# Second expert layer, block stage: GpSimd issues the 24 weight transfers instead of ScalarE

## The reference, cut to what matters

```python
E, K, F = (8, 2, 352)
scores = jax.nn.softmax(logits, axis=-1)
topk_w, topk_i = jax.lax.top_k(scores, K)
topk_w = topk_w / (topk_w.sum(-1, keepdims=True) + 1e-20) * SCALE
combine = jnp.zeros((T, E), jnp.float32).at[jnp.arange(T)[:, None], topk_i].set(topk_w)
g = jax.nn.silu(jnp.einsum('td,edf->etf', x, w_gate)) * jnp.einsum('td,edf->etf', x, w_up)
expert_out = jnp.einsum('etf,efd->etd', g, w_down)
y = jnp.einsum('te,etd->td', combine, expert_out).astype(x.dtype)
return y + _swiglu_mlp(identity, sw_gate, sw_up, sw_down)
```

## Time and profile before

| | us |
|---|---|
| median of 3 runs | 3525.72 |
| lowest and highest of them | 3525.45, 3530.16 |
| the profiled execution | 3523.55 |
| its span, first to last instruction | 3522.0 |
| block stage, first DMA issue to last result copy | 3055.65 to 3380.45 |

### The profile page before, as it was taken

How to read it: one execution, slowest core, us unless ns; L and a number is a source line. 1 busy time by engine, 2 the same in 40 slices (tenths; PEclk the granted TensorE clock), 3 DMA queues, 4 the chain that set the end, 5 groups by cost and what they waited for, 6 DMA issues and landing times. The chain is left out here.

```text
span 3522.0 us, 56185 instructions
## 1 busy us (share of the span) xinstructions
PE 3188.7 (91%) x17981; PEld 2290.7 (65%) x17982; DVE 2037.6 (58%) x4470; ACT 1273.8 (36%) x1786; POOL 1626.9 (46%) x933
## 2 busy tenths in 40 slices
PE   5875999999539999999999999999999957699988
PEld 4655888888536666666666666666666555477766
DVE  5656555555746666666766766666666662122235
ACT  2332333333434444444444444444444432122222
POOL 5002333333235666655666655666656636500037
PEclk8995999999769999999999999999999958899999
DMA  4000000001451111111111101111010031421223
GB/s 110 1 1 9 14 13 9 13 9 57 162 214 46 52 45 46 53 45 35 61 45 54 45 27 69 45 54 45 27 69 28 7 106 64 140 68 63 63 70 109
DMA packets 89978, 192.94 MB, mean 55 GB/s; under 512 B 12768, under 2 KB 58152, under 8 KB 83760
## 3 DMA queue, kind: packets, MB, share of 16 engines
q1 hardware_dynamic: 74864, 162.28, 13.1%
q0 software_dynamic: 10816, 21.07, 2.1%
q10 hardware_dynamic: 4224, 8.65, 0.7%
HBM read 137.60 MB, written 54.30 MB: 54 GB/s over the span
## 5 line engine op out<-in xcount | busy, mean ns | idle before, releaser
L2070 POOL TENSOR_TENSOR d_acc<-d_acc,d_pr 128x1024 f32<-128x1024 f32 x384 | 938.2, 2443 | 91.1 <-ACT d_pr L1974 60.4
L1974 ACT ACTIVATE d_pr<-d_p 128x1024 f32<-128x1024 f32 x512 | 487.0, 1026 | 236.2 <-PE d_p L1909 236.2
L1843 PE MATMUL d_pO<-d_pr,d_V 128*64 128x512 f32 x2048 | 473.0, 599 | 0.0
L2070 POOL TENSOR_TENSOR d_acc<-d_pr 128x1024 f32<-128x1024 f32 x64 | 153.1, 2392 | 620.9 <-ACT d_pr L1974 620.9
L2019 DVE TENSOR_REDUCE d_nm<-d_p 128x2 f32<-128x1024 f32 x256 | 304.6, 1222 | 94.9 <-PE d_p L1886 94.9
L2014 DVE CUSTOM_DVE_ANT_0 d_biased<-d_p,d_masked 128x512 f32<-128x512 f32 x512 | 330.6, 688 | 31.8 <-issue 31.8
L935 POOL TENSOR_TENSOR e_hs<-e_hf,e_hs 128x512 fp32r<-128x512 f32 x136 | 175.6, 1291 | 365.4 <-ACT e_hs L910 365.4
L1843 PEld LDWEIGHTS d_pO<-d_pr,d_V 128*64 128x64 f32 x2048 | 135.4, 136 | 261.5 <-issue 235.0
L965 DVE SCALAR_TENSOR_TENSOR res<-e_pY,m_Wt,res 128x256 f32<-128x256 f32 x544 | 225.9, 478 | 44.6 <-PE e_pY L871 43.8
L2030 DVE RECIPROCAL d_rb<-d_rb 128x128 f32<-128x128 f32 x256 | 224.6, 920 | 7.5 <-ACT d_rb L1967 7.5
L871 PEld LDWEIGHTS e_pY<-e_Wd,e_hs 128*128 128x128 f32 x1632 | 213.5, 191 | 13.8 <-POOL e_hs L935 2.2
(11 more groups left out here) (287 smaller groups left out, 5628.2 us busy)
## 6 DMA issues: line engine op xcount, KB each, us to landing
d_W<-w_split SPq DMA_DIRECT2D x32, 1536.0 KB, 6.4
kv_split<-c_ys SPq DMA_DIRECT2D x16, 1024.0 KB, 5.7
d_kv<-kv_split SPq DMA_DIRECT2D x8, 2048.0 KB, 10.6
d_masked<-mask_bias SPq DMA_DIRECT2D x64, 256.0 KB
x_slots<-m_zeros SPq DMA_DIRECT2D x1, 9088.0 KB, 29.7
b_x<-x_slots SPq DMA_DIRECT2D x71, 128.0 KB, 2.0
y_slots<-b_y SPq DMA_DIRECT2D x71, 128.0 KB, 1.7
w_split<-w_parts SPq DMA_DIRECT2D x4, 1536.0 KB, 5.3
```

What stands on the lines that cost most here:

```text
L1843: last = pe.matmul(pO[own[h], :], V[vb][:, s, par * P + h * HD1:par * P + (h + 1) * HD1], pr[:, s % PT, h, :], start=(s == 0), stop=(s == ...
L1974: act.activation(pr[:, n % PT, :, :], slot(st, what, n)[:, :, :], ACT.Exp).then_inc(exp_done, 1)
L2070: pool.tensor_tensor(acc[:, q, :, :], a, pr[:, s % PT, :, :], ALU.add).then_inc(acc_done, 1)
```

## The change

POOL issues the 24 weight transfers, and ACT issues none. POOL issues those of experts 0 and 1 first. Then, for each expert e, it issues those of expert e+2 (while there is one) and after that waits for expert e and marks it. Neither the transfers themselves, their semaphores, their order nor any wait of PE is changed.

```diff
             @block.gpsimd
             def _(pool):
+                def load(e):
+                    pool.dma_start(wgu[:, e, :, :], io["r1_gu"][:, e]).then_inc(w_in[e], 16)
+                    pool.dma_start(wd[:, e, 0:2, :], io["r1_d"][e, 0:2 * P].rearrange("(f p) d -> p f d", p=P)
+                                   ).then_inc(w_in[e], 16)
+                    pool.dma_start(wd[0:F1 - 2 * P, e, 2, :], io["r1_d"][e, 2 * P:F1]).then_inc(w_in[e], 16)
+
+                load(0)
+                load(1)
                 for e in range(E1):
+                    if e + 2 < E1:
+                        load(e + 2)
                     pool.wait_ge(w_in[e], 48)
                     pool.memset(told[:, e:e + 1], 0.0).then_inc(w_ready, 1)
...
             @block.scalar
             def _(act):
-                for e in range(E1):
-                    act.dma_start(wgu[:, e, :, :], io["r1_gu"][:, e]).then_inc(w_in[e], 16)
-                    act.dma_start(wd[:, e, 0:2, :], io["r1_d"][e, 0:2 * P].rearrange("(f p) d -> p f d", p=P)
-                                  ).then_inc(w_in[e], 16)
-                    act.dma_start(wd[0:F1 - 2 * P, e, 2, :], io["r1_d"][e, 2 * P:F1]).then_inc(w_in[e], 16)
-
```

## The result

| | before | after |
|---|---|---|
| median of 20 runs, us | 3525.46 | 3518.24 |
| lowest and highest | 3522.57, 3530.16 | 3513.43, 3524.32 |
| profiled execution, its span | 3523.55, 3522.0 | 3518.08, 3516.5 |

The ratio is 0.998, with a 95% interval of 0.9974 to 0.9986: faster by 7.2 us, where 12.3 were forecast. The time lies inside the stated range (3510 to 3519), close to its upper end, and just past the 7.1 us at which the prediction put the bound to no change.

The account below looks back on a forecast made before the run. PE's late start, set by ACT's list of DMA issues, was taken to bound the block stage, a fixed PE run of 305.3 us. First product 12.3 us earlier: 3525.72 - 12.3 = 3513.4 us, range 3510 to 3519.

Parts of the forecast that it names:

- the likeliest case: The forecast itself: gain 10.4 to 13.5 us, time 3512.2 to 3515.3, chance 0.68.
- rivals 1 and 2: POOL or its queue slower, gain 7.4 us, chance 0.12; blocks slower beside the weights, gain 6.3, chance 0.08.
- The start of PE: Block stage: PE's first product at 3062.9 instead of 3075.16, a gain of 12.3 us.
- The two bounds that were weighed: Mark 0 comes at the later of POOL finishing nine issues (3062.3) and expert 0's data landing (3062.5).
- POOL's issues: Ahead of mark 0: an expert's three issues take 2.13 us, nine 6.39, plus 0.27 for the first.
- I carry the same 305.3 us: First product to last result copy: the 71 blocks take as long as before, 305.3 us.
- Rival 2: Blocks run slower beside the weights: late row loads stall PE twice, 3.0 us each; gain 6.3, 3519.4 us; chance 0.08.
- The slack: SP's row loads: landing in 5.8 us at worst, needed after two blocks, 8.6 us; slack of 2.8 us.
- The clock: Block 0 again runs at the lower level (1.2 GHz); a rise one block later costs up to 3.8 us more.
- Later marks: POOL's marks after expert 0: up to 2.1 us later than their data, costed at nothing, covered by the blocks' length.
- Rivals 1 and 3: Nine POOL issues at 1.3 us, gain 7.4, chance 0.12; mark 0 behind stalled issues, up to 3549 us, chance 0.12.
- The two-port rule of the third rival: DVE in a two-port mode blocks GpSimd's DMA descriptors: nine issues 27.9 us, run 3534.5 us; chance 0.01.

Follow-up runs that it names:

- e5: The kernel before, with ACT's first copy of turned rows moved up behind expert 0's three transfers, ahead of the other 21; 3522.98 us, ratio 0.9994.
- e7: The changed kernel, with result stores issued by ACT and POOL pausing ahead of the loads of experts 3 to 7; 3512.83 us, ratio 0.9965.
- e6: The changed kernel, with POOL issuing all 24 transfers ahead of its first mark instead of nine; 3523.02 us, ratio 0.9992.
- e2: The changed kernel, with result stores issued by ACT behind its result copy, leaving SP only the row loads; 3515.95 us, ratio 0.9972.

## Why the prediction was right in direction and off in size

The point forecast, a gain of 12.3 us, missed, and so did the likeliest case, which ended at 3515.3. The median of 3518.24 lies inside the range because the range was opened upwards for rivals 1 and 2. By the mean of two profiles of each kernel the first product came 11.9 us earlier in the stage (19.2 against 7.3), and the blocks gave 3.7 back (305.2 against 308.9). The 13.5 at the upper end of the forecast gain has no term behind it; the bounds worked out were 13.0 and 10.4.

**The start of PE: right.** It was put 7.24 us after the stage's first issue; two profiles have 6.79 and 7.85. The two bounds that were weighed met as forecast: in both, the data set the mark and POOL's list ended 0.46 and 1.54 us earlier.

**POOL's issues: right in kind, 17% too dear** (2.13 us for one expert's three, 1.82 measured). This is the row for them that was missing (durations min/median/max in ns):

```profile
L1315 POOL DMA_DIRECT2D b_wgu<-in_r_gu_dram x8: 560/560/637, 3058.1 to 3077.5; - x8
L1316 POOL DMA_DIRECT2D b_wd<-in_r_d_dram x8: 724/724/776, 3058.7 to 3078.0; - x8
L1318 POOL DMA_DIRECT2D b_wd<-in_r_d_dram x8: 539/539/557, 3059.5 to 3078.7; - x8
```

0.56, 0.72 and 0.54 us where 0.68, 0.81 and 0.64 were worked out; nine took 5.56 us, not 6.66. The slope by rows fits (128 more rows cost 0.16 us; 0.13 was taken). One thing was wrong, by 0.5 us: POOL does not begin with ACT and SP, but 0.52 us after SP (0.51 or 0.52 in all six profiles in which it issues). The prediction had named a later start of POOL as a sign that it fails altogether; the sign came, too small to matter beside the 11.9 us.

**"I carry the same 305.3 us": wrong, and this is the step that failed.** The sum took the blocks as fixed. Rival 2 named what happened, with a gain of 6.3 us, and was given 0.08, by way of two stalls of 3.0 us where there was one of 1.90 or 1.50; the gain was 7.2 over the runs and 8.2 in the sum of the stage (mean of the two profiles of each kernel, 324.4 and 316.2). Two of its numbers were misread:

- The landing. The worst row load of the kernel before had landed in 5.8 us, but of its 71 loads only two were issued well inside the flow of weights (5.8 and 4.9 us); the median of 2.0 is that of a free queue. In the changed kernel five are, those of blocks 2 to 6. The traces of the changed kernel give no landings, those of other kernels give 4.8 to 7.5 us for such loads; the longest are 7.0 (e5, ACT's queue), 7.5 (e7) and 7.2 (e6, POOL's), here that of e6:

```profile
DMA to landing us min/median/max: 7.2/7.2/7.2
```

In the changed kernel the load of block 5 took 8.0 us, from 3079.17 to 3087.16. The Trainium skill (DMA: Bandwidth & Descriptors, "Queues, rings and completion order") says that each DMA engine takes turns between the queues that have work for it, packet by packet. The trace agrees only in part. These are e6's queues over the 4 us behind that load's issue (3079.55 to 3083.50), and then over the rest of it (to 3086.76; q0 is POOL's queue, q1 SP's):

```profile
q0 software_dynamic: 366, 1.39, 103.8%
```
```profile
q0 software_dynamic: 251, 0.99, 85.7%
q1 hardware_dynamic: 165, 0.15, 15.9%
```

For 4 of its 7.2 us the load moved no packet at all, and then both queues moved together (SP's 165 packets are its 144 and the first of the load behind it). It did not wait for all that POOL had issued before it: a weight transfer issued at 3073.92 landed at 3088.76, 2.0 us after the load. In the changed kernel SP's queue likewise moved nothing from 3079.17 to 3082.90, and then four transfers at once. In the kernel before the load at 3080.31 had its first packet 3.0 us after its issue, and where no weights flow a queue moves its first packet about 0.9 us after an issue. Whether the first packets are made late or served late no run shows.

- The slack. I counted two blocks, 8.6 us, from the turn of block j to the need of block j+2. But SP's list is in order: ahead of the load of block 5 stands the store of block 0, and that waits for the first result copy. The load went out at 3079.17, 2.7 us after the turn that released it (3076.44), and was needed at 3085.26: 6.1 us of slack against 8.0 of landing. The prediction named ACT's and POOL's lists and not SP's. The store also put its 128 KB into the same queue ahead of the load (e2). In the kernel before the same order did no harm, because SP's load of block 5 came at 3090.16, when the weights had landed.

**The clock: right for block 0, missing behind the stall.** Block 0 ran at the lower level as carried, but its length was not fixed: 5.0 to 6.1 us from its first product to the next block's in nine profiles (all but e5), by the moment at which the clock rose; the sum carried the 5.9 of one. The drop after a new gap (six down products in 2.92 us instead of 1.46 in one profile, none in the other) had no term.

**The rest.** Later marks cost nothing, as forecast: POOL issued between them and waited for data each time. Rivals 1 and 3 fell with the issue times above. The two-port rule of the third rival could not be tried at its place, since DVE was idle there. Of the 15 later issues four overlapped a DVE instruction (24 in the five profiles in which POOL issues between its marks), and none was longer than 0.56, 0.72 and 0.54 us. That is no test of the rule either: these instructions are products of two sources and copies out of PSUM, and no trace shows whether any ran in a two-port mode.

Why the row loads under the flow spread from 4.8 to 8.0 us stays open. What is left of the median (7.2 measured, 8.2 by the stage) is within what the start of the stage varies by, and the longer end of the two profiles of the changed kernel would take a part of it too.

## What to carry to other kernels

A late start that is traced to the length of one engine's list of issues can be removed by moving or by spreading the list, and the issuing engine hardly matters (7.28 us with ACT, 6.79 and 7.85 with POOL); but everything that shares the list counts, and moving one victim out of it (the copy) without the other (Silu) gains next to nothing. When work starts earlier it meets transfers that used to be over: take the landing time from loads that were issued under the same flow, not from the median, and read the slack from the order of the queue that issues them. A simple remedy is to let no store stand ahead of a load whose data are needed first.

## What the runs showed of the hardware

- A transfer issued by GpSimd took 0.54 to 0.78 us of its time, and 24 in a row were never held up; on ScalarE the first of a stage took 1.8 us, most of the others 0.33 to 0.7, and with all 24 in one list single ones from about the 17th on up to 2.55.
- Expert 0's 1.06 MB were marked 6.0 to 7.1 us after POOL's first issue (five profiles, four of them at most 6.5) and 6.8 to 7.1 after ACT's (four), of which ACT's first issue alone is 1.8 and POOL's 0.64: loads of this size came no later by GpSimd.
- A 128 KB load that lands in 2.0 us alone took 4.8 to 8.0 us beside a flow of weights of about 350 GB/s. In four such loads (the kernel before, e2, e6, the changed kernel) 3.0 to 4.1 us went by before its queue moved a first packet.
- Gaps of 1.90 and 2.40 us in PE's work were each followed by a stretch at a granted clock of 0.50 (1.2 GHz), one of 1.50 us was not (three profiles, one gap in each).
